# Dealing a layer's small VectorE operations to other steps of the attention loop, and starting GpSimd's affine later

## The reference

```python
x = x + attention(_gn(x), ...)              # 8 heads of 64, all 1024 pixels against all
x = x + deformable_attention(_gn(x), ...)   # layer norm over channels, 16 windows of 8 x 8
```

```python
off = tanh(einsum('bchw,oc->bohw', gelu(conv(gq)), off_pw_w)) * 4
vgrid = 2 * (grid + off) / (n - 1) - 1
kv = _grid_sample(xp, vgrid)                       # bilinear: products of hats max(0, 1 - |x - ix|)
pos = qgrid - vgrid
bias = mlp(sign(pos) * log1p(abs(pos)))            # three layers, two relus
out = softmax(q k^T / 8 + bias) v
```

## Time and profile before

| | us |
|---|---|
| median of 3 runs | 3061.41 |
| lowest and highest run | 3054.13, 3062.18 |
| the profiled execution's own time | 3059.49 |
| its span, first to last instruction | 3057.7 |

### The profile page before, as it was taken

One profiled execution on the slowest core, in us unless ns is written; L12 is line 12 of the kernel. 1 busy time (PEld: TensorE's weight loads), 2 busy tenths in 40 slices (PEclk: granted clock), 3 DMA queues, 4 the chain that ended last, 5 costly groups with the idle time before them and its releaser, 6 DMA issues.

```text
span 3057.7 us, 59737 instructions
## 1 busy us (share of the span) xinstructions
PE 2820.7 (92%) x24696; PEld 1962.0 (64%) x24696; DVE 2210.2 (72%) x2934; ACT 1657.9 (54%) x2429; POOL 196.7 (6%) x157
## 2 busy tenths in 40 slices
PE   6999799999999999999999999999999999997858
PEld 4676577756766577665677567675676656765434
DVE  5676587587875787767876778768787587775756
ACT  2563466374663656535664556537566275653534
POOL 0000011000200002000020001100020000200300
PEclk9999899999999999999999999999999999999968
DMA  5233023311235022340124211232123401114030
GB/s 198 65 74 111 28 46 105 118 60 44 62 91 166 8 61 58 105 145 21 50 59 147 94 42 46 76 138 69 44 58 95 158 16 55 38 24 158 14 106 28
DMA packets 149598, 235.79 MB, mean 77 GB/s; under 512 B 78609, under 2 KB 97556, under 8 KB 145460
## 3 DMA queue, kind: packets, MB, share of 16 engines
q1 hardware_dynamic: 148468, 219.39, 23.2%
q10 hardware_dynamic: 864, 12.58, 1.2%
HBM read 177.08 MB, written 54.84 MB: 76 GB/s over the span
## 4 chain that ended last, share of the span: by engine, by line
PE 71%; DVE 12%; DMA 6%; ACT 4%; issue 4%; SPq 2%; another core or an unknown queue 0%; DVEq 0%; POOL 0%; ACTq 0%
PE banks L695 12%; PE banks L635 10%; PE banks L664 10%; PE banks L682 8%; PE banks L625 6%; PE banks L874 5%; PE banks L737 4%; PE banks L884 4%; PE banks L875 3%; PE banks L876 3%; DMA point_outputs_dram<-point_outputs 3%; DVE neg_max L1411 2%; ACT exps L1092 2%; DVE exps_turned L1420 2%; PE banks L847 2%
## 5 line engine op out<-in xcount | busy, mean ns | idle before, releaser
L1411 DVE TENSOR_REDUCE neg_max<-banks 128x1 f32<-128x1024 f32 x512 | 601.8, 1217 | 96.1 <-PE banks L664 95.4
L1092 ACT ACTIVATE exps<-banks,neg_max 128x1024 f32<-128x1024 f32 x512 | 567.2, 1114 | 43.6 <-DVE neg_max L1411 42.6
L1102 ACT ACTIVATE exps_turned<-banks 128x1024 f32<-128x1024 f32 x256 | 262.5, 1026 | 543.8 <-PE banks L682 539.8
L1420 DVE COPY exps_turned<-banks 128x1024 f32<-128x1024 f32 x256 | 313.2, 1223 | 261.5 <-PE banks L682 255.1
L664 PE MATMUL banks<-qk_halves 64*128 64x512 f32 x3072 | 434.6, 415 | 68.1 <-ACT exps L1092 50.5
L695 PE MATMUL banks<-exps_turned,values 128*64 128x256 f32 x4096 | 479.8, 384 | 0.8 <-issue 0.8
L682 PEld LDWEIGHTS banks<-ident,exps 64*128 64x128 f32 x8192 | 311.4, 140 | 194.5 <-issue 167.2
L682 PE MATMUL banks<-ident,exps 64*128 64x64 f32 x8192 | 366.8, 229 | 25.5 <-DVE exps_turned L1420 24.4
L664 PEld LDWEIGHTS banks<-qk_halves 64*128 64x128 f32 x3072 | 293.5, 190 | 119.0 <-issue 83.5
L695 PEld LDWEIGHTS banks<-exps_turned,values 128*64 128x64 f32 x4096 | 279.7, 137 | 138.0 <-issue 4.0
L1589 DVE SCALAR_TENSOR_TENSOR qk_halves<-banks,qk_halves 128x1024 fp32r<-128x1024 f32 x256 | 301.7, 1218 | 88.2 <-ACT qk_halves L1141 88.0
(11 more groups left out here) (183 smaller groups left out, 3346.0 us busy)
## 6 DMA issues: line engine op xcount, KB each, us to landing
wqk_ring<-wqk_split SPq DMA_DIRECT2D x62, 512.0 KB, 4.5
wo_halves<-wo_split_dram SPq DMA_DIRECT2D x8, 2048.0 KB, 7.8
exps_turned<-in_x SPq DMA_DIRECT2D x32, 512.0 KB, 6.0
x_dram<-exps SPq DMA_DIRECT2D x32, 512.0 KB, 2.6
exps_turned<-x_dram SPq DMA_DIRECT2D x32, 512.0 KB, 6.2
out<-exps_turned SPq DMA_DIRECT2D x32, 512.0 KB, 2.9
recips_b<-recips_dram SPq DMA_DIRECT2D x240, 64.0 KB, 3.5
x_image<-in_x SPq DMA_DIRECT2D x14, 1024.0 KB, 6.9
```

What stands on the lines that cost most here:

```text
L1092: freed(act.activation(PB[:, 2 * h + n % 2], slot(("s", m, i)), ACT.Exp, bias=NM[:, m:m + 1], accum_out=SS[:, m:m + 1]), ("s", m, i))
L1411: dve.tensor_reduce(NM[:, m:m + 1], slot(("s", m, i)), AX.X, ALU.max, negate=True).then_inc(mx, 1)
L1420: dve.tensor_copy(PT[:, n // 2 % 2, 1, :, P * j:P * j + P].rearrange("p k (r q) -> p k r q", r=2), TB.rearrange("p r (k q) -> p k r q", k= ...
```

## The change

The operations themselves stay as they are. Sample points and log inputs move from step 5 to step 6, ScalarE's logarithm from step 5 to step 7, the log split from step 7 to step 10, all six log rows from steps 8 to 13 into step 14, and the hats from step 6 to step 18. SyncE's transfers of the log rows follow pair 7 in place of pair 6. GpSimd's affine waits for 40 maxima in place of 28. The end of the kernel, where the last image's second layer runs alone, is untouched.

```diff
@@ sync
-                    if u == 6 and i:
+                    if u == 7 and i:
                         rows_to_dram(i - 1)
@@ gpsimd
                 if i + 1 < B:
-                    pool.wait_ge(mx, (i + 1) * TILES + 28)
+                    pool.wait_ge(mx, (i + 1) * TILES + 40)
@@ scalar
-                    if i and n == 5:
+                    if i and n == 7:
                         log(i - 1)
@@ vector
-                    if i and n == 5:
+                    if i and n == 6:
                         sample_points(i - 1)
                         log_inputs(i - 1)
-                    if i and n == 6:
+                    if i and n == 10:
+                        log_split(i - 1)
+                    if i and n == 14:
+                        for part in range(3):
+                            for o in range(2):
+                                log_row(part, o, i - 1)
+                    if i and n == 18:
                         hats(i - 1)
-                    if i and n == 7:
-                        log_split(i - 1)
-                    if i and 8 <= n < 14:
-                        log_row((n - 8) // 2, (n - 8) % 2, i - 1)
                     copy_turned(n, i)
```

## The result

The changed kernel takes 3097.05 us (median of 6 runs, 3079.12 to 3104.8), the kernel before, run beside it, 3061.8 (6 runs, 3054.13 to 3064.56): a ratio of 1.0109 with the 95% interval 1.0078 to 1.0141, slower. The profiled execution of the changed kernel took 3100.86 us for a span of 3098.6, at a mean granted clock of 0.961 in place of 0.967; 41.4 us more than the profiled one before.

A forecast was written before the change was run, and what follows sets the result against it. TensorE, busy 92%, was taken as the bound, VectorE counting only where TensorE waits. From 3059.49 us: +27.3 (hats), +14 (clock), -1.5 (step 7), -2 (late copies) = 3097; range 3060 to 3112.

The forecast's parts named there:

- The hats beside GpSimd: Step 18: four of five hats each wait for an affine instruction, TensorE 3.9 us late per image, +27.3 us.
- the worked chain: Step 18: five dependent hats beside the affine end at 6.17 us, 4.36 us more than alone.
- The clock: Behind step 18's stall: TensorE's granted clock falls, 2.0 us per stall between bounds 0 and 3.1, +14 us in all.
- Step 7's wait: Step 7: TensorE's 0.21 us wait for the copy goes once the log split leaves, -1.5 us over seven images.
- The logarithm's table load: Steps 6 and 8: ScalarE's reload of the exponentials' table moves TensorE's 0.53 us gap to step 8, sum 0.
- Log split in step 10: Step 10: the split's 1.72 us fits into 2.03 us of idle time before the copy, cost 0.
- Log rows in step 14: Step 14: six log rows, 1.69 us, fit into 2.23 us of room as GpSimd no longer runs there, cost 0.
- The rows' transfers: SyncE's queue: taken as 0; as a rival, blocking ScalarE in step 18, 3063 to 3070 without the hats' stall, chance 0.03.
- Late copies that find the stall already there: Just after step 18: late samples and copies are hidden by the stall, an estimated -2 us.
- partly blocked hats: Rival, steps 18 and 21: only some hats blocked, or step 21's statistics meet the affine's end; 3064 to 3076, chance 0.15.
- nothing collides: Rival, step 18: hats win each hand-over, only step 7's gain is left, 3056 to 3059, chance 0.10.
- faster: Rival: late copies come from VectorE's crowding by the even spread; half of 24.4 us goes, 3047, chance 0.06.

The follow-up runs named there:

- run 2: Changed kernel with GpSimd's affine released by 42 maxima in place of 40, a step after the hats: 3072.94 us, ratio 1.0030 to the kernel before.
- run 5: Changed kernel with each affine instruction of GpSimd cut into two of 128x256: 3079.59 us, ratio 1.0049 to the kernel before.
- run 1: Changed kernel with GpSimd's affine released by 28 maxima again, so it runs beside step 14's log rows: 3112.11 us, ratio 1.0159 to the kernel before.
- run 7: Changed kernel with twelve more matmuls on TensorE ahead of step 19's first turn, in the stall: 3087.68 us, ratio 1.0075 to the kernel before.
- run 3: Changed kernel with log rows in steps 11 to 13, hats in step 14, transfers after pair 6, affine from 33 maxima: 3066.3 us, ratio 1.0006.
- run 4: Kernel before with one edit, GpSimd's affine released by 40 maxima in place of 28: 3062.12 us, ratio 1.0002.

## Why the prediction was right, step by step

- **The hats beside GpSimd** (+27.3 us): the mechanism is shown, by the rows of step 18 and from both sides by runs 2 and 5: without the meeting each hat is as long as alone, and with half the instruction the waiting is halved. In none of the nine traces is a VectorE instruction more than 0.6 us longer than the shortest of its form unless it meets the affine. The size was 4 us too large: 3.33 us an image, 23.3 together. I priced a blocked hat at 1.42 us, from the ends of two neighbours in the earlier trace rows, and measured were 1.27, 1.19 and 1.21. The affine's plain 1.28 us, from the earlier trace rows, would have been the better price, as run 1 shows too (1.30 for each of six log rows). With it the worked chain would have been three times 0.14 us shorter, 5.75 us against 5.74 measured. That is 2.9 of the 4 us; the rest is at the two ends, where the first hat and the copy each start 0.08 us before the row ahead of them ends. I had expected affine instructions of 1.45 us between the hats; the first four took 1.26 to 1.33.
- **The clock** (+14): 13.8 measured in step 19, and shown by run 7, where it goes with TensorE's idle time. I had taken 2.0 us between the bounds 0 and 3.1; the seven images gave 2.7, 2.9, 1.6, 0, 2.8, 2.5 and 1.3. So it is a mean over a scatter, and the images don't agree on one price. By the length of TensorE's wait: behind 1.1 us (run 5) the clock fell in no image, behind 3.3 us in six of seven, behind 4.7 to 5.7 us (run 1) in all. The 13.8 are those of the profiled execution. The six runs of the changed kernel lie 26 us apart, 3079.12 us at a mean granted clock of 0.966 and 3104.8 at 0.960, while the kernel before's lie 10 us apart; so the term probably changes from run to run, but only one of the six has a trace.
- **Step 7's wait** (-1.5): gone, as the first row below shows, and the step is 0.18 us shorter in the mean (0.05 to 0.24), -1.3.
- **The logarithm's table load** (0): the gap went from step 6 to step 8 (0.57 us ahead of the scores there). Steps 6 and 8 together: 13.71 before, 13.57 after, -0.9 over the images. TensorE's timeline, the turn that the earlier trace rows has waiting and the scores in step 8:

```profile
414.24 0.71 PE L682 MATMUL banks<-ident,exps 64*128 64x64 f32 x16
...
419.77 1.66 PE L664 MATMUL banks<-qk_halves 64*128 64x512 f32 x12 [0.57 <-ACT exps L1092]
```

- **Log split in step 10** (0): it fits; in four images its copy still has 0.70 us of idle time ahead of it. In the other three the copy starts 0.6 to 1.0 us later than that, which the profile doesn't explain; that is the step's +2.8.
- **Log rows in step 14** (0): they fit where the affine isn't (no such wait in run 3 either, with two in a step); run 1 shows the price where it is.
- **The rows' transfers** (0): the first is issued at 471.38 and all have landed 4.1 to 5.3 us after the first issue, in the second image at 476.63, 4 us before ScalarE's copy of step 18 starts. No wait of ScalarE for them is in the trace, and that rival falls.
- **Late copies that find the stall already there** (-2): not shown. Step 20, which takes samples of the next image, is 3.7 us shorter in sum, the expected sign, but in run 4, which has no stall of hats in step 18, it is 3.5 us shorter too. In the trace of before 2.5 of the 3.7 are one image, where VectorE waits for the transfer of a sample, and neither the changed kernel's trace nor run 4's has such a wait in step 20:

```profile
1952.82 0.69 DVE L1355 BATCH_NORM_STATS2 bn_stats<-probs_or_sample 128x6 f32<-128x512 f32 x1 [3.56 <-DMA probs_or_sample<-in_x]
```

- **The rivals**: partly blocked hats fall by the rows by tile, "nothing collides" by the same, "faster" by run 3. Step 21 doesn't pay in the changed kernel, as the affine is over before that step's statistics in every image. That 3097 was met to the microsecond is luck in part: the hats were 4 us over, the -2 has no shown cause, 7.4 us in steps 24 to 30 and at the end were in no term, and the runs themselves spread over 26 us.

No version tried here beats the kernel before; the third and the fourth equal it.

## What to carry to other kernels

When VectorE's small operations out of SBUF are moved, look first at what GpSimd does at that moment: beside this affine each one behind the first cost up to a whole GpSimd instruction of 1.2 to 1.3 us, whatever its own size, and a step's room must be counted in those. A later affine that costs nothing alone (run 4) and hats that cost nothing in another step (run 3) cost 1% together, so ask of every moved piece what else now starts on the same event. And a stall's price isn't over when it ends: behind 3.3 us of it TensorE's clock took another 2 us in the mean.

## What the hardware showed that I had not expected

- Shorter GpSimd instructions halve the wait in one place and starve VectorE in another. A tensor_tensor of 128x4, 0.16 us alone, took 7.48 us in one image beside instructions of 128x128, many of which passed it, and 3.44 and 3.62 us in two images beside those of 128x256. With 128x512 no VectorE instruction in any trace lost more than 1.25 us, one turn. Why some lose one turn and others many stays open.
- Cut into quarters, the affine as a whole became longer: its instructions sum to 224 us in the whole program in place of 168, at 0.46 to 0.49 us each for a quarter of what takes 1.28.
- After seven stalls of the same 3.30 us, behind the same instructions, the clock fell in six images and not in one. What sets it apart the runs don't show.
